# A planned decoder kernel without its filler matmuls on TensorE

## The reference, cut to what matters

```python
x = x + _L0_attn_ref(_layernorm(x), ...)    # ternary weights, quantised rows, rotary, 16 heads of 8, causal softmax
x = x + _L0_xattn_ref(ctx, ctx, _layernorm(x), mask, ...)   # attention to a text of 64 rows per sequence
x = x + _L0_ffn_ref(_layernorm(x), ...)     # 8 experts, top 2 of them per token: silu(x w1) * (x w3), times w2
x = x + _L1_attn_ref(_layernorm(x), ...)    # linear causal attention with gates, no softmax
x = x + _L1_xattn_ref(_layernorm(x), ctx)   # adds the most similar text row
x = x + _L1_ffn_ref(_layernorm(x), ...)     # 128 -> 512 -> 128, piecewise-linear GELU on fixed-point values
```

## Time and profile before

| | |
|---|---|
| time, median of 3 runs | 378.13 us (373.85 to 378.9) |
| the profiled execution: time, span in the profile | 378.12 us, 375.4 us |
| TensorE busy | 330.0 us (88%), 4932 matmul records, of them 300 fillers |
| VectorE, ScalarE, GpSimd busy | 236.6, 171.9, 141.3 us |
| mean granted clock of TensorE | 0.955 of full speed |

### The profile page before, as it was taken

How to read it: one execution, slowest core, us unless ns; L and a number is a source line. 1 busy time by engine, 2 the same in 40 slices (tenths; PEclk the granted TensorE clock), 3 DMA queues, 4 the chain that set the end, 5 groups by cost and what they waited for, 6 DMA issues and landing times.

```text
span 375.4 us, 12711 instructions
## 1 busy us (share of the span) xinstructions
PE 330.0 (88%) x4932; PEld 262.6 (70%) x4932; DVE 236.6 (63%) x786; ACT 171.9 (46%) x492; POOL 141.3 (38%) x173
## 2 busy tenths in 40 slices
PE   0999999999997998998978778999997779996865
PEld 0435867877766897988957767999995557964644
DVE  4796685778886661327683124636479686767772
ACT  1389334234342253444434336675466087816040
POOL 5193441135518041325485187423353660101000
PEclk9999999999999599999899999999999899999696
DMA  8760000000003618075466676545540200000000
GB/s 271 299 237 2 6 2 4 3 3 3 3 9 90 239 29 270 28 256 175 164 194 238 212 234 210 175 138 171 158 141 14 50 23 2 8 11 3 0 14 14
DMA packets 19724, 38.51 MB, mean 103 GB/s; under 512 B 2129, under 2 KB 13009, under 8 KB 19538
## 3 DMA queue, kind: packets, MB, share of 16 engines
q1 hardware_dynamic: 17458, 34.62, 28.1%
q0 software_dynamic: 1024, 2.10, 1.8%
q10 hardware_dynamic: 1184, 0.99, 0.8%
HBM read 29.98 MB, written 7.73 MB: 100 GB/s over the span
## 4 chain that ended last, share of the span: by engine, by line
PE 57%; issue 13%; POOL 9%; DVE 9%; DMA 6%; ACT 4%; SPq 1%; POOLq 0%; ACTq 0%; DVEq 0%
PE Op L866 11%; PE FU L686 10%; PE AC L695 5%; PE Sp L795 4%; PE FU L809 4%; PE FU L978 3%; PE Mp L970 2%; POOL yr L622 2%; POOL hh L590 2%; POOL xg L612 2%; PE Sp L809 2%; PE Qp L740 2%; POOL rstd L584 1%; DMA x<-in_x 1%; DMA wbuf<-in_w 1%
## 5 line engine op out<-in xcount | busy, mean ns | idle before, releaser
L590 POOL TENSOR_TENSOR hh<-hh,uu 128x256 f32<-128x256 f32 x60 | 43.4, 733 | 70.4 <-DVE hh L1500 70.2
L686 PE MATMUL FU<-xgT,wbuf 128*128 128x128 f32 x480 | 63.9, 282 | 1.9 <-DVE hh L1500 1.4
L686 PEld LDWEIGHTS FU<-xgT,wbuf 128*128 128x128 f32 x480 | 59.3, 196 | 4.7 <-DVE hh L1500 1.7
L584 POOL TENSOR_TENSOR rstd<-powed,minus_half 128x1 f32<-128x1 f32 (+1 forms) x36 | 22.8, 636 | 74.3 <-DVE powed L1192 55.4
L1500 DVE SCALAR_TENSOR_TENSOR hh<-th,FU 128x256 f32<-128x256 f32 x60 | 24.7, 419 | 30.1 <-ACT uu L995 28.2
L1005 ACT ACTIVATE th<-FU 128x256 f32<-128x256 f32 x60 | 23.5, 392 | 42.0 <-PE FU L686 41.9
L584 POOL TENSOR_TENSOR rms<-rms,minus_half 128x20 f32<-128x20 f32 x8 | 28.4, 3546 | 28.5 <-DVE rms L1287 28.5
L695 PE MATMUL AC<-wbuf,hh 128*128 128x128 f32 x240 | 32.7, 279 | 6.6 <-POOL hh L590 5.5
L695 PEld LDWEIGHTS AC<-wbuf,hh 128*128 128x128 f32 x240 | 29.3, 192 | 9.1 <-issue 7.6
L978 PE MATMUL FU<-causal_b,identb 128*128 128x384 bf16 x144 | 34.7, 353 | 0.0
L1340 DVE TENSOR_REDUCE mpad<-Sp 128x8 f32<-128x512 f32 x32 | 20.6, 687 | 12.3 <-PE Sp L795 12.0
(11 more groups left out here) (261 smaller groups left out, 691.3 us busy)
## 6 DMA issues: line engine op xcount, KB each, us to landing
wbuf<-in_w SPq DMA_DIRECT2D x30, 768.0 KB, 4.7
xg<-zeros SPq DMA_DIRECT2D x2, 2048.0 KB, 10.3
xg<-xg SPq DMA_DIRECT2D x30, 64.0 KB, 2.4
yg<-ys SPq DMA_DIRECT2D x30, 64.0 KB, 4.4
params<-in_params SPq DMA_DIRECT2D x1, 1632.0 KB, 10.5
x<-in_x ACTq DMA_DIRECT2D x1, 512.0 KB, 4.6
text<-in_ctx SPq DMA_DIRECT2D x1, 512.0 KB, 7.0
out<-x SPq DMA_DIRECT2D x4, 128.0 KB, 1.8
```

Source lines behind the costliest of these rows:

```text
L584: return nc.gpsimd.tensor_tensor(o, base, exponent[:, 0:o.shape[1]], ALU.pow)
L590: nc.gpsimd.tensor_tensor(hh[:, u % NB, :], hh[:, u % NB, :], uu[:, u % NB, :], ALU.mult)\
L686: ins = mm(FU[:, v % 2, 256 * part + P * i:256 * part + P * i + P], wbuf[:, u % WB, c:c + P], xgT[:, u % 2, :], start=True, stop=True)
```

## The change

One line of `plan()` goes: the filler is no longer appended. The three lines behind it stay, so the plan's own clock for TensorE still runs as if the filler were issued, and every other stage comes at the same point of the plan.

```diff
@@ -301,7 +301,6 @@
                 rested = [(freed.get(name, 0.0), k) for k, name in enumerate(SPARE) if not full.get(name)]
                 if not rested or min(rested)[0] > now - REST:
                     continue
-                order[e].append(("keep_warm", min(rested)[1]))
                 free_at[e] = now + WARM
                 fill_at = now + PACE
                 events.append((free_at[e], 1, ()))
```

## The result

| | before | without fillers |
|---|---|---|
| median of 5 runs | 378.9 us (373.85 to 382.14) | 405.22 us (404.17 to 411.16) |
| ratio | | 1.078, 95% interval 1.070 to 1.086 |
| span of the profiled execution | 375.4 us | 407.3 us |
| mean granted clock | 0.955 | 0.843 |
| fillers | 300 | 0 |

The kernel became 7.8% slower, 26 us in the medians and 31.9 us between the two profiled executions. The forecast was 394 us, range 380 to 409.

What follows compares the result with a forecast made beforehand. TensorE bounds 35 to 94 us; GpSimd, DMA and issue lead from 175 to 235; engines alternate from 284. Terms 3.4 + 4.6 + 0 + 0 + 6.9 + 1 = +15.9 on 378.12 give 394 us, own range 387 to 402, stated 380 to 409.

Steps and rivals of the forecast that it cites:

- the rival in which the clock stays down: Whole kernel: at the low clock it may not rise again; about 417 us, milder forms from 403; chance 0.17.
- the fillers counted as gained: Chain time freed by removed fillers: 6.3 us at the start, 3.1 in the attention, half of 2.6 from 284 us.
- The price of the low clock: Attention's chain: L866 +81%, L809 +67%; 0.45 us lost per us at low clock where TensorE is the bound.
- The start: 9 to 36 us: clock low until 28 us, +8.0 and +1.7, less 6.3 of fillers: +3.4 us, bounds -6.3 to about +6.
- Attention, 35 to 94 us: Three clock falls, 17 us together, cost +7.7, fillers give -3.1: +4.6 us, bounds -4.1 to +26.
- 94 to 131 us: Routing on VectorE and GpSimd leads, so 0; +2 if TensorE's share were lost too.
- Experts: 131 to 284 us: GpSimd and DMA work covers the low clock; sum 0, bounds -2 to +6 us.
- 284 to 346 us: Two thirds of a wholly low clock's 12.3 us lost, half the fillers' 2.6 gained: +6.9 us, bounds -2.6 to +12.
- The end: 346 us on: both `zout` already pay the low clock; only L959 and two transposes can double: +1 us.
- The faster case: Whole kernel: fillers were in the way, half of some 17.5 us on the chain comes free: 369 us; chance 0.08.
- The real work holds the clock: Rival: packed real work keeps the clock; start -3, attention -3, loss only from 284 us on: 380 us; chance 0.2.

Runs made afterwards that it cites:

- light fillers: All 300 fillers kept in the kernel before, each on 32 rows and 32 columns of the array; ratio 1.165 (1.147 to 1.182), median 447.4 us.

## Why the prediction was right, and where it was not

**How near it came.** 405 us lies in the stated 380 to 409, but above the forecast's own 387 to 402, and the rival in which the clock stays down put its milder forms there too (from 403 us on). The forecast change was 10 us too small, and one kind of term makes up that much: the fillers counted as gained, 6.3 + 3.1 + 1.3 = 10.7 us. The losses alone were forecast at 26.6 us, and 26.3 were measured in the medians. That this is so close is partly luck, as the terms below show.

**The direction and the mechanism** held: the loss is the low clock, in the start, the attention and the tail, and nothing from 175 to 281 us (delay 25.15 to 25.29).

**The price of the low clock** held: L865 took 3.52 us for 64 records (3.57 forecast), L808 1.92 (1.82 forecast). The 0.45 us lost for each low us was an estimate for places where TensorE is the bound, and it is too much for the whole kernel. The mean clocks give 128 us low after and 34 before, and the starts ahead of the first record add 34 and 5 us; 0.45 of the difference of 123 us is 55 us, an estimate, where 31.9 were measured, 0.26 us for each. L865 and L808 grew by 79 and 76%, and part of the low work is off the chain.

**The start, +3.4 forecast, +9.1 measured**, is the term that was mis-sized, and 9.1 is outside its own bounds (about +6). Its losses were 8.0 + 1.7 = 9.7 us, near the 9.1. The error is the other half: the 6.3 us of fillers in the chain of the earlier trace rows were counted as gained. They gave nothing: the delay at 13.4 us is +0.09. A chain puts a filler down whenever no wait shows behind it, and the wait that it covered came out in its place, `textT` in the rows above. The clock stayed low until 44 us, not 28, but that cost little: the delay is 7.9 us at 30.0 and 9.1 us at 38.1.

**Attention, 35 to 94 us: +4.6 forecast, +7.1 measured** (9.09 to 16.17). Not three falls of 5.7 us but one of 3.4 and one of 17.1: TensorE was busy 16.17 of the 17.1 us, with L865 and L808 in it, and the clock stayed at 0.50. Count and price were near; the length was the mean of falls in a kernel with fillers, and the longest of those is 10.2 us. The losses were forecast at 7.7 us, near the measured 7.1. The 3.1 us of fillers counted as gained are not to be seen: the delay nowhere steps back by more than 0.8 us. The size also differs from trace to trace: without the attention's fillers the same stretch gave 4.4 us behind a start with fillers, and 11.9 with only the first 38. So a miss of 2.5 us is less than one profile can tell.

**94 to 131 us: 0 forecast, +2.0 measured**, at the bound of +2 that was given.

**Experts: 0 forecast, +7.1 measured**, all between 143.8 and 176.5 us. By the kernel without just these fillers they are worth 0.3%, interval -0.4 to 1.0. So the forecast was right on average and wrong for this profile, where 7.1 is outside its bounds (-2 to +6). The profile of the kernel without its tail's fillers has 7.7 us of the same kind there, with all of the experts' fillers in place.

**284 to 346 us: +6.9 forecast, +7.1 measured**, though by other pieces. I had L866 as the largest part; the two that stand in the end of the chain ran at full clock (1.91 for 62 records, 2.03 us for 64), and L808 and L958 paid (start us, length us). The kernels without the tail's fillers and with only the first 38 have 5.0 and 6.8 us over the same stretch.

```profile
325.29 2.05 PE Qp L958 x4
336.50 1.99 PE Sp L808 x64
362.49 2.03 PE Op L865 x64
371.23 2.05 PE Qp L958 x4
384.59 3.75 PE Mp L969 x16
399.67 3.77 PE Mp L969 x16
```

**The end: +1 forecast, -0.4 measured.** The last `zout` is as slow as before, 3.77 against 3.75 us, as forecast. The last L958, which was to double, ran at full clock between two low stretches: 1.10 us, at 389.3 us.

**The rivals.** The faster case is out, and with it the reading that fillers on the chain cost their length. "The real work holds the clock" is out for the attention by the kernel with only the first 38; among the experts, from 242 us on, it did. What its chance of 0.2 held besides, a loss at the start alone, is out too: of the delay of 31.93 us at 367.7 us, 9.09 stand at 38.1 us. The case that the clock stays down came true in part, for 17 us in the attention and 27 in the tail.

## What to carry to other kernels

A filler in the chain of waits is worth its length only if nothing that it covered was about to end (6.3 us of them stood in the start's chain, and without them no matmul came more than 0.09 us earlier); compare the start of the next real instruction without it before counting a gain. Check that a filler does its work: of the three kinds tried only the full one (128x128 weights, 384 columns) held the clock, at a mean of 0.955 against 0.840 and 0.842. On 32x32 of the array, or with 8 columns, the kernel was slower than without any (ratios 1.165 and 1.105 against 1.078). And they belong in the waits ahead of expensive TensorE work on the chain, as many as the wait is long: 22 ahead of the last `zout` left 4.6 us idle and the `zout` took 3.75 us; with 48, and more in the waits ahead of it, it took 2.02 to 2.04 us in all four profiles. Over the whole kernel that gave 0.1 and 0.8% in two measurements.

## What was not expected

In 8 of the 14 profiled executions, TensorE stalled for some 5 to 7 us between 115 and 145 us (in one of them, light fillers, from 163 us), in the middle of the same 64 matmuls of L809, which wait for nothing but their turn. From the first start to the last they take 0.98 us in the kernel before and 6.2 to 7.7 us in these eight. Here is TensorE of the kernel without the first 38 fillers, where that line is L812:

```profile
124.14 0.79 PE L812 MATMUL FU<-qT,keys 64*64 64x64 f32 x34
125.33 0.31 PE L812 MATMUL FU<-qT,keys 64*64 64x64 f32 x2 [0.39 <-issue]
126.06 0.21 PE L812 MATMUL FU<-qT,keys 64*64 64x64 f32 x1 [0.42 <-issue]
126.78 0.28 PE L812 MATMUL FU<-qT,keys 64*64 64x64 f32 x2 [0.51 <-issue]
128.20 0.25 PE L812 MATMUL FU<-qT,keys 64*64 64x64 f32 x1 [1.15 <-issue]
...
131.09 0.95 PE L812 MATMUL FU<-qT,keys 64*64 64x64 f32 x22 [1.06 <-issue]
```

GpSimd issues eight indirect scatters in that time, the first at 119.56 us and the last here; the DMA engines' share is 0.13 to 0.14 up to 127 us and 0.92 from 129.6 us, when the experts' first weights load:

```profile
128.63 0.96 POOL L615 DMA_INDIRECT xg<-xall,slot  x1 [0.30 <-issue]
```

The scatters alone do not bring it: the kernel before issues the same eight from 110.63 to 120.67 us and has no stall. Nor is it a matter of the kernel. The kernel with 60 more fillers in the tail was profiled twice, its scatters start at 110.7 and 110.6 us, and the first execution has no stall and the second has:

```profile
115.31 1.19 PE L816 MATMUL FU<-qT,keys 64*64 64x64 f32 x64
```

```profile
115.21 0.73 PE L816 MATMUL FU<-qT,keys 64*64 64x64 f32 x33
116.39 0.33 PE L816 MATMUL FU<-qT,keys 64*64 64x64 f32 x3 [0.46 <-issue]
117.84 0.28 PE L816 MATMUL FU<-qT,keys 64*64 64x64 f32 x2 [1.11 <-issue]
```

The delay grows by 7 to 9 us where the stall comes; in three of the eight some 4 to 5 us of it are won back by 136 us of the kernel before. The clock is low in or behind it, but in the kernel before the clock also falls at 120.4 us without a stall. Neither the kernel before nor the changed one shows the stall in its own profile, so it is no part of the change; it can add to the spread of any of these kernels. What holds the instructions back was not tried.
